# The five engine lists of a two-layer Macaron kernel, put in another order

## The chip, the cores and the metric

The kernel runs on one core of a Trainium2 chip. The metric is the device time of one launch in microseconds (us). The core has five engines, each with its own instruction list that it works off strictly in order: TensorE (PE: matmuls and transposes), VectorE (DVE), ScalarE (ACT), GpSimd (POOL) and SyncE (SP, which only issues transfers). Engines wait for one another through semaphores; whatever stands behind a waiting instruction in the same list waits too.

## The reference, cut to what matters

Two layers over 4096 tokens of width 128, in float32. Each layer is a middle block between two halves: layer 0 is a gated recurrence between two quantized linear maps, layer 1 a gated linear attention between two passes of a mixture of experts (8 routed, the best 2 per token, and a shared one):

```python
x = x + 0.5 * quant(ln(x));  x = x + recur(ln(x));  x = x + 0.5 * quant(ln(x))     # layer 0
x = x + 0.5 * experts(ln(x)); x = x + attend(ln(x)); x = x + 0.5 * experts(ln(x))   # layer 1
# recur
t  = rmsnorm(x) ; xb = causal_depthwise_conv(t @ Wx)
r, i = sigmoid(xb @ Wa), sigmoid(xb @ Wi)
a  = exp(-8 * softplus(lam) * r)
h  = scan(a, sqrt(max(1 - a*a, 1e-12)) * (i * xb))
h1 = x + (h * gelu(t @ Wy)) @ Wo
y  = h1 + (gelu(u @ Wg) * (u @ Wu)) @ Wd          # u = rmsnorm(h1)
# quant: x rounded to int8 by row, times the int8 weight, scaled, plus bias
# attend: state = state * g_t + k_t v_t^T ; o_t = q_t state ; out = o @ Wo + bo
# experts: (silu(x @ Wg.T) * (x @ Wu.T)) @ Wd.T, top 2 of 8, weighted, plus a shared one
```

## The kernel before, in words

The tokens are eight units (`u` = 0 to 7) of 512 tokens (4 tiles of 128). All of `x` stays in on-chip memory. The kernel is written as small steps, each a function named `<step>_<engine>`, and the order of the steps on each engine is written out in five blocks at the end of the kernel (lines 1486 on): `block.sync`, `vector`, `scalar`, `gpsimd`, `tensor`. Steps of many units and phases are interleaved there. The waits are inside the steps, so the order of a list changes nothing of what is computed; it decides what queues behind what. Letters of the steps:

- `k_`: constants and loads. `k_masks` turns masks to bytes on ACT, `k_split` splits the quantized weight on POOL.
- `q_` (u, p): the quantized map, pass p. `q_stats`, `q_limits`, `q_mom`, `q_par`, `q_scale`, `q_whole` and `q_out` on DVE, `q_root` and `q_bias` on POOL, `q_turn` and `q_mul` on PE, `q_copy` on ACT.
- `f_` (u): the recurrence block. On POOL `f_root`, `f_rstd`, `f_apply` (normalized x into h1, four instructions), `f_b` (the scan's input), `f_xh`, `f_root2`; on DVE `f_mom`, `f_conv`, `f_scan` (waits for `f_b`), `f_hy`; the rest on PE and ACT.
- `m_` (u, j): its feed-forward part. `g_` (u): the attention, with seven `g_level` steps on PE and DVE; `g_bias` on POOL adds a bias to `x`, `g_root` a power for the norm, `g_gate` a gate on ACT, `g_first` starts the levels.
- `r_` (u, p): the router. `r_slot` gives each token its place; `r_scatter` (POOL, four steps of two indirect transfers) writes the tokens, sorted by expert, to `rows_by_expert` in HBM. `e_` (u, p): the shared expert.
- `x_` (p, j): the routed experts, tile j of 71 in each pass; pass 0 is before the attention, pass 1 after it. The lists give p first for these, as in `x_hid_vector(dve, 0, j)`. `t_load` and `t_weights` (SP) fetch the tile's tokens (`tin`, 65 KB, ring of 12) and weights (`twt`, 256 KB, ring of 4). `x_io j` on PE first does the down projection of tile j-5 and then transposes tile j. `x_up j` is the up and gate projection, `x_silu` and `x_out` are on ACT, `x_hid` is the product on DVE, and `t_store` (POOL) scatters the result to `rows_done`. From tile 49 on, `x_dst` (DVE, 128x1, line 1113) first works out where a tile's rows go.
- The tiles come in waves that start at tiles 0, 9, 25, 41 and 49: `table p,w` on DVE computes which experts the tiles of wave w belong to, and `t_load` of its first tile waits for it and for the scatters of the units of that wave. `away` and `taken` are small tables.
- `t_stored`, `c_fetch` (SP, 512 KB a unit) and `c_add` (DVE) bring the results back and add them to `x`; `o_store` writes the output. `x_up 70`, for example, is tile 70 of the pass spoken of.

The step `x_hid`, on whose queueing much depends (lines 1116 to 1122):

```python
            dve.wait_ge(s_tsil, g + 1)
            if g >= TURNS:
                dve.wait_ge(s_tdn, g - TURNS + 1)
            dve.tensor_tensor(thidt[g % TURNS][:, :, :].rearrange("p j c -> p (j c)"), tsil[g % TURNS][:, :],
                              bank[UP_BANKS[p][j]][:, INNER:2 * INNER], ALU.mult).then_inc(s_thid, 1)
```

## Time and profile before

| | us |
| --- | --- |
| median of 3 runs | 793.06 (793.04 to 793.74) |
| span of the profiled execution (first to last instruction) | 692.3 |
| whole time of the profiled execution | not recorded; the median is 100.8 above the span |
| busy in the span: PE / DVE / POOL / ACT | 600.1 / 497.2 / 419.3 / 387.7 |
| mean granted TensorE clock | 0.972 of full |

Busy time is the union of the instructions of an engine. An engine of 87% can still be the bound for long, and one of 61% can be it for a stretch; so the rows below are read by stretches of the span.

### The profile page before, as it was taken

To read this page: it belongs to the slowest core of one execution; us is meant where nothing else is said; L and a number is where in the kernel's file an instruction comes from. 1 tells how busy PE (TensorE), PEld (TensorE's weight loads), DVE (VectorE), ACT (ScalarE), POOL (GpSimd) and SP (SyncE) were. 2 spreads that over 40 slices of the span, in tenths; PEclk is the share of its full clock that TensorE was granted. 3 is DMA by queue.
4 is the path that set the end of the run, shared out by engine and by line. 5 is a ranking of instruction groups with operands and counts; after the bars stand their busy time and mean duration, and the time that the engine had idled before them with its cause. 6 is when DMAs were issued, how large, how long until landed. Compare 5 with 4: busy or idle time off the path is not lost.

```text
span 692.3 us, 14370 instructions
## 1 busy us (share of the span) xinstructions
PE 600.1 (87%) x4124; PEld 476.3 (69%) x4124; DVE 497.2 (72%) x1721; ACT 387.7 (56%) x1019; POOL 419.3 (61%) x445
## 2 busy tenths in 40 slices
PE   0366999999989998999897899999999999978974
PEld 0224565655666797888696686769879989857863
DVE  7997999978998865557224798989877766553335
ACT  2395968988766545444353728466565355533541
POOL 5276696488567777567643614553776575775552
PEclk9996999999999999999999999999999999999997
DMA  7999000001033355666768600124216556566796
GB/s 258 410 411 371 0 1 1 1 0 32 13 99 94 97 156 161 186 193 180 211 176 245 235 6 1 35 66 131 74 43 172 153 151 177 161 182 189 231 297 232
DMA packets 60125, 100.97 MB, mean 146 GB/s; under 512 B 10288, under 2 KB 28592, under 8 KB 59792
## 3 DMA queue, kind: packets, MB, share of 16 engines
q1 hardware_dynamic: 50832, 81.52, 38.5%
q0 software_dynamic: 8640, 17.84, 7.4%
q8 instruction: 35, 0.57, 0.4%
q10 hardware_dynamic: 576, 0.69, 0.3%
q14 instruction: 42, 0.34, 0.2%
HBM read 61.79 MB, written 38.23 MB: 144 GB/s over the span
## 4 chain that ended last, share of the span: by engine, by line
PE 43%; DVE 13%; DMA 9%; issue 6%; POOL 3%; SPq 2%; ACT 2%; POOLq 0%; DVEq 0%; ACTq 0%
PE bank L1083 13%; PE bank L1058 6%; PE bank L1296 5%; DMA tin<-rows_by_expert 3%; PE bank L969 3%; PE bank L955 3%; PE bank L944 2%; DMA hid<-rows_done 2%; DMA rows_done<-tout,tdst 2%; PE bank L1064 2%; DMA rows_done<-tout,tin 1%; POOL rows_by_expert L840 1%; DVE qt L417 1%; PE bank L312 1%; PE bank L307 1%
## 5 line engine op out<-in xcount | busy, mean ns | idle before, releaser
L840 POOL DMA_INDIRECT rows_by_expert<-xx,sidx x128 | 128.1, 1001 | 72.2 <-issue 34.0
L1083 PE MATMUL bank<-tint,twt 128*128 128x128 f32 x1136 | 151.8, 282 | 6.0 <-DVE thidt L1121 3.4
L1083 PEld LDWEIGHTS bank<-tint,twt 128*128 128x128 f32 x1136 | 141.1, 196 | 22.0 <-issue 12.3
L1132 POOL DMA_INDIRECT rows_done<-tout,tin x98 | 96.3, 983 | 57.5 <-ACT tout L1107 34.8
L1121 DVE TENSOR_TENSOR thidt<-tsil,bank 128x256 f32<-128x256 f32 x142 | 58.2, 418 | 95.8 <-ACT tsil L1099 74.1
L1099 ACT ACTIVATE tsil<-bank 128x256 f32<-128x256 f32 x142 | 53.9, 384 | 89.9 <-PE bank L1083 88.4
L1058 PE MATMUL bank<-e_dn,thidt 128*128 x568 | 90.6, 286 | 15.5 <-DVE thidt L1121 7.3
L1058 PEld LDWEIGHTS bank<-e_dn,thidt 128*128 128x128 f32 x568 | 76.8, 195 | 25.2 <-issue 24.8
L1107 ACT ACTIVATE tout<-bank,tin 128x128 f32<-128x128 f32 x142 | 50.2, 366 | 62.9 <-PE bank L1064 43.7
L1132 POOL DMA_INDIRECT rows_done<-tout,tdst x44 | 43.7, 993 | 49.0 <-ACT tout L1107 35.9
L1296 PEld LDWEIGHTS bank<-bufA,bufB 128*127 128x127 f32 (+6 forms) x448 | 47.7, 176 | 11.6 <-issue 6.7
L1296 PE MATMUL bank<-bufA,bufB 128*127 128x127 f32 (+6 forms) x448 | 52.2, 263 | 3.7 <-DVE bufA L1272 1.8
L1092 ACT ACTIVATE tint<-bank 128x128 f32<-128x128 f32 x142 | 37.1, 274 | 27.6 <-PE bank L1064 27.3
L1064 PE MATMUL bank<-consts,tin 128*128 128x128 f32 x142 | 39.5, 282 | 6.4 <-DMA tin<-rows_by_expert 6.4
L687 PE MATMUL bank<-ut,w_gu 128*128 128x512 f32 x64 | 34.4, 620 | 1.7 <-DVE hid L696 1.7
L673 PE MATMUL bank<-ut,w_gu 128*128 128x512 f32 x64 | 34.5, 621 | 1.0 <-DVE x L709 1.0
L955 PE MATMUL bank<-xtr,s_gu 128*128 128x512 f32 x64 | 34.0, 614 | 0.9 <-ACT egate L951 0.9
L944 PE MATMUL bank<-xtr,s_gu 128*128 128x512 f32 x64 | 33.3, 603 | 0.4 <-DVE carry L809 0.3
L969 PEld LDWEIGHTS bank<-e_dn,ehid 128*128 128x128 f32 x256 | 30.1, 192 | 3.1 <-DVE ehid L963 1.7
L969 PE MATMUL bank<-e_dn,ehid 128*128 128x128 f32 x256 | 31.4, 276 | 0.8 <-DVE ehid L963 0.8
L963 DVE TENSOR_TENSOR ehid<-egate,bank 128x512 f32<-128x512 f32 x32 | 21.9, 684 | 13.2 <-PE bank L955 8.4
L951 ACT ACTIVATE egate<-bank 128x512 f32<-128x512 f32 x32 | 19.1, 596 | 20.5 <-PE bank L944 20.4
(272 smaller groups left out, 1331.0 us busy)
## 6 DMA issues: line engine op xcount, KB each, us to landing
twt<-moe_gu SPq DMA_DIRECT2D x142, 256.0 KB
rows_by_expert<-tout SPq DMA_DIRECT2D x25, 715.0 KB, 20.0
tin<-rows_by_expert SPq DMA_DIRECT2D x142, 65.0 KB, 2.6
hid<-rows_done SPq DMA_DIRECT2D x12, 512.0 KB, 5.5
x<-x_in SPq DMA_DIRECT2D x8, 256.0 KB, 4.4
rows_by_expert<-xx,sidx POOLq DMA_INDIRECT x128
out<-x SPq DMA_DIRECT2D x8, 256.0 KB, 3.9
rows_done<-tout,tin POOLq DMA_INDIRECT x98
```

The source lines that it names most:

```text
L840: pool.indirect_dma_start(out=rows_by_expert, out_offset=bass.IndirectOffsetOnAxis(ap=sidx[h][:, k:k + 1], axis=0), in_=xx[h][:, r, t, :], ...
L944: pe.matmul(bank[E_BANKS[p]][:, :], s_gu[:, 0, j * P:(j + 1) * P], xtr[u % 2][:, :], start=True, stop=True).then_inc(s_sg, 1)
L955: pe.matmul(bank[E_BANKS[p]][:, :], s_gu[:, 1, j * P:(j + 1) * P], xtr[u % 2][:, :], start=True, stop=True).then_inc(s_su, 1)
L969: m = pe.matmul(bank[E_BANKS[p]][:, t * P:(t + 1) * P], ehid[u % 2][:, j, t * P:(t + 1) * P], e_dn[:, SHARED, j, :], start=(j == 0), stop= ...
L1058: m = pe.matmul(bank[b][:, P:2 * P], thidt[g % TURNS][:, c, :], e_dn[:, expert_pe[j], c, :], start=(c == 0), stop=(c == IJ - 1))
L1064: pe.transpose(bank[b][:, 0:P], tin[g % RING][:, 0:D], ident).then_inc(s_tt, 1)
L1083: m = pe.matmul(bank[UP_BANKS[p][j]][:, c * P:(c + 1) * P], weights[:, c * P:(c + 1) * P], tint[g % TURNS][:, :], start=True, stop=True)
L1099: act.activation(tsil[g % TURNS][:, :], bank[UP_BANKS[p][j]][:, 0:INNER], ACT.Silu).then_inc(s_tsil, 1)
L1107: act.activation(tout[:, g % RING, :], bank[IO_BANKS[p][j + LAG_DOWN]][:, P:2 * P], ACT.Copy, scale=tin[g % RING][:, ROW_SCORE:ROW_SCORE + ...
L1121: dve.tensor_tensor(thidt[g % TURNS][:, :, :].rearrange("p j c -> p (j c)"), tsil[g % TURNS][:, :], bank[UP_BANKS[p][j]][:, INNER:2 * INNE ...
L1132: pool.indirect_dma_start(out=rows_done, out_offset=bass.IndirectOffsetOnAxis(ap=dst, axis=0), in_=tout[:, g % RING, :], in_offset=None).t ...
L1296: m = pe.matmul(gb(u, lv % 2)[0:P - w, c * P + w:(c + 1) * P], bufB[h][:, c * P:(c + 1) * P - w], bufA[h][:, c * P + w:(c + 1) * P], start ...
```

## The change

The steps, their waits and their buffers are the same: each of the five lists holds the same steps as before. Only their order is new: SP 316 steps, DVE 636, POOL 293, PE 704, ACT 745. Most move by one to five places; 2 on SP, 45 on DVE, 7 on POOL, 22 on PE and 47 on ACT move by more. The order was planned with the durations of single instructions and with transfers taken at their 85th percentile. The diff has some 3,200 lines; here are the places that the prediction speaks of, in the order SP (end of the first pass, end of the second), DVE (table of the first pass, turn of the passes, end), POOL (head, 300 to 390 us), PE (second pass, tiles 45 to 49) and ACT (286 us).

```diff
             c_fetch_sync(sp_, 0, 0)
             c_fetch_sync(sp_, 1, 0)
-            for j in range(65, 67):
+            t_load_sync(sp_, 0, 66)
+            c_fetch_sync(sp_, 2, 0)
+            for j in range(67, 69):
                 t_load_sync(sp_, 0, j)
-            t_weights_sync(sp_, 0, 65)
-            for j in range(67, 70):
-                t_load_sync(sp_, 0, j)
-            for j in range(66, 69):
+            for j in range(64, 68):
                 t_weights_sync(sp_, 0, j)
+            t_load_sync(sp_, 0, 69)
+            c_fetch_sync(sp_, 3, 0)
+            t_weights_sync(sp_, 0, 68)
+            c_fetch_sync(sp_, 4, 0)
             t_load_sync(sp_, 0, 70)
-            c_fetch_sync(sp_, 2, 0)
-            c_fetch_sync(sp_, 3, 0)
...
+            t_load_sync(sp_, 1, 66)
+            t_weights_sync(sp_, 1, 65)
+            t_load_sync(sp_, 1, 67)
             t_weights_sync(sp_, 1, 66)
+            t_load_sync(sp_, 1, 68)
+            t_weights_sync(sp_, 1, 67)
+            t_load_sync(sp_, 1, 69)
+            t_weights_sync(sp_, 1, 68)
             t_stored_sync(sp_, 1, 0)
             c_fetch_sync(sp_, 0, 1)
-            for j in range(68, 71):
-                t_load_sync(sp_, 1, j)
-            for j in range(67, 70):
-                t_weights_sync(sp_, 1, j)
+            t_load_sync(sp_, 1, 70)
             c_fetch_sync(sp_, 1, 1)
             c_fetch_sync(sp_, 2, 1)
-            t_weights_sync(sp_, 1, 70)
             c_fetch_sync(sp_, 3, 1)
             c_fetch_sync(sp_, 4, 1)
             c_fetch_sync(sp_, 5, 1)
+            for j in range(69, 71):
+                t_weights_sync(sp_, 1, j)
+            o_store_sync(sp_, 0)
+            o_store_sync(sp_, 1)
             t_stored_sync(sp_, 1, 6)
             c_fetch_sync(sp_, 6, 1)
-            o_store_sync(sp_, 0)
-            o_store_sync(sp_, 1)
-            o_store_sync(sp_, 2)
             t_stored_sync(sp_, 1, 7)
             c_fetch_sync(sp_, 7, 1)
+            o_store_sync(sp_, 2)
             o_store_sync(sp_, 3)
...
-            for j in range(29, 33):
+            for j in range(28, 30):
                 x_hid_vector(dve, 0, j)
             e_hid_vector(dve, 6, 0, 0)
-            for j in range(33, 35):
+            r_slot_vector(dve, 7, 0)
+            table_vector(dve, 0, 4)
+            for j in range(30, 33):
                 x_hid_vector(dve, 0, j)
-            table_vector(dve, 0, 4)
-            x_hid_vector(dve, 0, 35)
             e_hid_vector(dve, 6, 0, 1)
-            for j in range(36, 40):
-                x_hid_vector(dve, 0, j)
+            x_hid_vector(dve, 0, 33)
...
-            g_stats_vector(dve, 2)
-            for j in range(67, 69):
-                x_dst_vector(dve, 0, j)
             c_add_vector(dve, 3, 0)
             g_stats_vector(dve, 3)
-            x_dst_vector(dve, 0, 69)
             c_add_vector(dve, 4, 0)
-            for j in range(67, 69):
-                x_hid_vector(dve, 0, j)
+            x_hid_vector(dve, 0, 67)
+            g_stats_vector(dve, 4)
+            x_hid_vector(dve, 0, 68)
+            g_stats_vector(dve, 2)
             g_mom_vector(dve, 1)
             g_value_vector(dve, 0)
             g_first_vector(dve, 0)
@@ -2086,26 +2066,29 @@
             g_level_vector(dve, 1, 2)
             g_level_vector(dve, 0, 3)
             g_level_vector(dve, 1, 3)
+            x_dst_vector(dve, 0, 65)
             g_level_vector(dve, 0, 4)
             g_level_vector(dve, 1, 4)
-            x_hid_vector(dve, 0, 69)
             g_level_vector(dve, 0, 5)
-            x_dst_vector(dve, 0, 70)
             g_level_vector(dve, 1, 5)
             g_level_vector(dve, 0, 6)
             g_level_vector(dve, 1, 6)
-            x_hid_vector(dve, 0, 70)
-            g_stats_vector(dve, 4)
...
-            for j in range(62, 68):
+            for j in range(61, 64):
+                x_hid_vector(dve, 1, j)
+            for j in range(64, 67):
                 x_dst_vector(dve, 1, j)
+            for j in range(64, 66):
+                x_hid_vector(dve, 1, j)
+            for j in range(67, 71):
+                x_dst_vector(dve, 1, j)
+            for j in range(66, 71):
+                x_hid_vector(dve, 1, j)
             c_add_vector(dve, 0, 1)
-            for j in range(64, 67):
-                x_hid_vector(dve, 1, j)
             c_add_vector(dve, 1, 1)
-            for j in range(68, 70):
-                x_dst_vector(dve, 1, j)
-            for j in range(67, 69):
-                x_hid_vector(dve, 1, j)
             c_add_vector(dve, 2, 1)
-            for j in range(69, 71):
-                x_hid_vector(dve, 1, j)
-            x_dst_vector(dve, 1, 70)
+            e_hid_vector(dve, 7, 1, 1)
             c_add_vector(dve, 3, 1)
-            e_hid_vector(dve, 7, 1, 1)
...
             k_first_gpsimd(pool)
             q_root1_gpsimd(pool, 0)
+            k_split_gpsimd(pool)
             q_root1_gpsimd(pool, 1)
             q_bias_gpsimd(pool, 0, 0)
-            k_split_gpsimd(pool)
             q_bias_gpsimd(pool, 1, 0)
             f_root_gpsimd(pool, 0)
             q_root_gpsimd(pool, 1, 0)
             q_root_gpsimd(pool, 2, 0)
             q_bias_gpsimd(pool, 2, 0)
-            q_bias_gpsimd(pool, 3, 0)
             f_rstd_gpsimd(pool, 0)
             f_apply_gpsimd(pool, 1)
+            q_bias_gpsimd(pool, 3, 0)
             f_apply_gpsimd(pool, 0)
             f_b_gpsimd(pool, 0)
             f_root_gpsimd(pool, 1)
+            q_bias_gpsimd(pool, 4, 0)
             f_b_gpsimd(pool, 1)
+            f_root2_gpsimd(pool, 0)
+            f_root2_gpsimd(pool, 1)
+            f_rstd_gpsimd(pool, 1)
+            q_root_gpsimd(pool, 3, 0)
+            q_bias_gpsimd(pool, 5, 0)
             f_xh_gpsimd(pool, 0)
...
+            for j in range(31, 38):
                 t_store_gpsimd(pool, 0, j)
-            r_scatter_gpsimd(pool, 7, 0, 1)
             r_scatter_gpsimd(pool, 7, 0, 2)
             r_scatter_gpsimd(pool, 7, 0, 3)
-            for j in range(37, 61):
+            for j in range(38, 62):
                 t_store_gpsimd(pool, 0, j)
             g_root_gpsimd(pool, 0)
-            for j in range(61, 65):
+            for j in range(62, 64):
                 t_store_gpsimd(pool, 0, j)
             g_bias_gpsimd(pool, 0)
             g_bias_gpsimd(pool, 1)
-            for j in range(65, 67):
+            for j in range(64, 66):
                 t_store_gpsimd(pool, 0, j)
...
-            x_up_tensor(pe, 1, 44)
-            x_io_tensor(pe, 1, 48)
             x_up_tensor(pe, 1, 45)
+            for j in range(47, 49):
+                x_io_tensor(pe, 1, j)
+            x_up_tensor(pe, 1, 46)
             x_io_tensor(pe, 1, 49)
-            x_up_tensor(pe, 1, 46)
+            x_up_tensor(pe, 1, 47)
             x_io_tensor(pe, 1, 50)
-            x_up_tensor(pe, 1, 47)
-            for j in range(51, 53):
-                x_io_tensor(pe, 1, j)
...
                 x_silu_scalar(act, 0, j)
-            x_out_scalar(act, 0, 18)
-            for j in range(23, 25):
+            for j in range(21, 23):
                 x_in_scalar(act, 0, j)
+            x_out_scalar(act, 0, 16)
+            e_silu_scalar(act, 5, 0, 0)
             x_silu_scalar(act, 0, 21)
+            r_tanh_scalar(act, 6, 0)
+            x_silu_scalar(act, 0, 22)
+            x_in_scalar(act, 0, 23)
+            for j in range(17, 20):
+                x_out_scalar(act, 0, j)
             r_apply_scalar(act, 7, 0)
```

## Rows read from the trace of the kernel before

**Rows 1.** Windows of the whole span: busy time of each engine.
```profile
core 0: us, PE busy (x) PEld busy (x) DVE busy (x) ACT busy (x) POOL busy (x), PEclk, DMA share, GB/s
0.00:70.00 70.00, 29.67 (x141) 17.77 (x142) 57.60 (x216) 35.79 (x73) 35.98 (x56) 0.90 0.92 358
70.00:225.00 155.00, 148.30 (x796) 93.61 (x796) 139.28 (x443) 122.77 (x261) 109.21 (x109) 0.98 0.09 27
225.00:345.00 120.00, 110.90 (x846) 95.83 (x845) 71.25 (x275) 56.60 (x179) 84.70 (x88) 0.99 0.60 169
...
400.00:600.00 200.00, 195.42 (x1498) 166.80 (x1497) 160.75 (x578) 110.09 (x311) 113.58 (x117) 1.00 0.34 98
...
650.00:693.00 43.00, 26.58 (x192) 23.58 (x191) 18.16 (x44) 12.63 (x41) 16.62 (x18) 0.90 0.76 255
```

**Rows 2.** Timeline of POOL near 319 us: start, duration, instruction, idle before.
```profile
319.30 0.95 POOL L1132 DMA_INDIRECT rows_done<-tout,tin  x1 [0.30 <-issue]
```

**Rows 3.** Groups by line, ACT: count, busy us, mean ns, idle before.
```profile
L577 ACT ACT_TABLE_LOAD x6 | 7.7, 1283 | 0.1
```

**Rows 4.** Timeline of POOL, 37 to 55 us.
```profile
37.92 1.28 POOL L425 TENSOR_TENSOR x<-x,half_qb 128x512 f32<-128x512 f32 x1
42.57 1.27 POOL L425 TENSOR_TENSOR x<-x,half_qb 128x512 f32<-128x512 f32 x1 [3.37 <-DVE qt L417]
43.79 1.83 POOL L339 TENSOR_TENSOR lf_rstd<-lf_ve,neg_half 128x8 f32<-128x8 f32 x1
45.73 7.43 POOL L619 TENSOR_SCALAR h<-x,lf_mean,lf_rstd 128x128 f32<-128x128 f32 x8
53.13 1.26 POOL L589 TENSOR_TENSOR bufB<-bufD,bufB 128x512 f32<-128x512 f32 x1
```

**Rows 5.** Timeline of DVE, 51 to 58 us.
```profile
51.20 0.16 DVE L474 TENSOR_SCALAR ms<-lf_var 128x8 f32<-128x8 f32 x1
54.42 1.27 DVE L597 TENSOR_TENSOR_SCAN bufE<-bufA,bufB 128x256 f32<-128x256 f32 x2 [3.06 <-POOL bufB L589]
...
56.95 0.86 DVE L318 BATCH_NORM_STATS2 lq_stats<-x 128x6 f32<-128x128 f32 x4
```

**Rows 6.** Timeline of POOL, 289 us.
```profile
289.88 0.96 POOL L1132 DMA_INDIRECT rows_done<-tout,tin  x1 [3.48 <-ACT tout L1107]
```

**Rows 7.** Timeline of ACT, 288 us (two `x_out` steps).
```profile
288.70 0.81 ACT L1107 ACTIVATE tout<-bank,tin 128x128 f32<-128x128 f32 x2
```

**Rows 8.** Timeline of DVE, 305 to 318 us.
```profile
305.83 0.74 DVE L1121 TENSOR_TENSOR thidt<-tsil,bank 128x256 f32<-128x256 f32 x2
...
311.64 0.16 DVE L873 TENSOR_TENSOR cnt<-carry,consts 128x8 f32<-128x8 f32 x1
...
317.37 0.24 DVE L895 SCALAR_TENSOR_TENSOR rtab<-stab,base,consts 128x22 int32<-128x22 f32 x1
```

**Rows 9.** Timeline of ACT, 312 us (`x_out 30` and `31`).
```profile
312.06 0.62 ACT L1107 ACTIVATE tout<-bank,tin 128x128 f32<-128x128 f32 x2
```

**Rows 10.** Tile `tdst`: duration in ns, min/median/max, first and last start.
```profile
L1113 DVE TENSOR_TENSOR tdst<-tin,away_of x44: 143/152/2570, 344.1 to 678.6; 128x1 int32<-128x1 int32 x44
```

**Rows 11.** Timeline of POOL, 391 us.
```profile
390.86 2.52 POOL L1194 TENSOR_TENSOR x<-x,rows 128x512 f32<-128x512 f32 x2
```

**Rows 12.** Timeline of PE, 628 to 631 us.
```profile
628.77 0.33 PE L1064 MATMUL bank<-consts,tin 128*128 128x128 f32 x1 [1.91 <-DMA tin<-rows_by_expert]
628.93 1.23 PE L1083 MATMUL bank<-tint,twt 128*128 128x128 f32 x8
```

**Rows 13.** Timeline of DVE, 672 to 690 us.
```profile
672.13 0.69 DVE L1161 TENSOR_TENSOR x<-x,hid 128x512 f32<-128x512 f32 x1 [5.45 <-DMA hid<-rows_done]
...
678.28 0.42 DVE L1121 TENSOR_TENSOR thidt<-tsil,bank 128x256 f32<-128x256 f32 x1 [1.68 <-PE bank L1058]
...
688.41 0.69 DVE L1161 TENSOR_TENSOR x<-x,bufC 128x512 f32<-128x512 f32 x1 [2.53 <-DMA bufD<-rows_done]
```

**Rows 14.** Timeline of SP, 664 us; then the page's DMA issues.
```profile
664.37 0.33 SPq L1029 DMA_DIRECT2D twt<-moe_gu  x1
664.75 0.90 SPq L1156 DMA_DIRECT2D hid<-rows_done  x2
...
twt<-moe_gu SPq DMA_DIRECT2D x142, 256.0 KB
...
hid<-rows_done SPq DMA_DIRECT2D x12, 512.0 KB, 5.5
```

**Rows 15.** Windows, 670 to 675 us, columns as in rows 1.
```profile
670.00:675.00 5.00, 1.99 (x15) 1.80 (x14) 2.81 (x8) 1.12 (x4) 2.14 (x2) 0.91 0.99 364
```

More of the change, by code:

```diff
@@ L2096, in _ @@
             g_level_vector(dve, 1, 6)
-            x_hid_vector(dve, 0, 70)
-            g_stats_vector(dve, 4)
+            for j in range(69, 71):
+                x_hid_vector(dve, 0, j)
+            for j in range(66, 70):
+                x_dst_vector(dve, 0, j)
+            c_add_vector(dve, 5, 0)
+            r_start_vector(dve, 1)
             g_add_vector(dve, 0)
@@ L2508, in _ @@
             r_scatter_gpsimd(pool, 6, 1, 3)
-            for j in range(28, 38):
+            for j in range(30, 38):
                 t_store_gpsimd(pool, 1, j)
@@ L2711, in _ @@
             e_up_tensor(pe, 2, 0, 1)
-            for j in range(5, 7):
+            for j in range(4, 6):
                 x_io_tensor(pe, 0, j)
@@ L2715, in _ @@
             e_down_tensor(pe, 2, 0)
-            x_io_tensor(pe, 0, 7)
+            for j in range(6, 8):
+                x_io_tensor(pe, 0, j)
             r_turn_tensor(pe, 4, 0)
@@ L3108, in _ @@
             x_up_tensor(pe, 1, 27)
-            x_io_tensor(pe, 1, 29)
+            for j in range(29, 31):
+                x_io_tensor(pe, 1, j)
             r_turn_tensor(pe, 6, 1)
@@ L3112, in _ @@
             r_logits_tensor(pe, 6, 1)
-            x_io_tensor(pe, 1, 30)
+            x_io_tensor(pe, 1, 31)
             x_up_tensor(pe, 1, 29)
-            for j in range(31, 33):
+            for j in range(32, 34):
                 x_io_tensor(pe, 1, j)
@@ L3408, in _ @@
             r_apply_scalar(act, 5, 0)
-            for j in range(8, 10):
-                x_in_scalar(act, 0, j)
+            x_in_scalar(act, 0, 8)
+            q_copy_scalar(act, 6, 1)
             x_out_scalar(act, 0, 4)
@@ new lines, in _ @@
+            x_in_scalar(act, 0, 11)
+            for j in range(7, 9):
+                x_out_scalar(act, 0, j)
+            x_in_scalar(act, 0, 12)
+            e_silu_scalar(act, 4, 0, 1)
+            for j in range(9, 12):
+                x_silu_scalar(act, 0, j)
+            r_tanh_scalar(act, 5, 0)
+            x_silu_scalar(act, 0, 12)
+            for j in range(13, 15):
+                x_in_scalar(act, 0, j)
+            x_out_scalar(act, 0, 9)
+            for j in range(15, 17):
+                x_in_scalar(act, 0, j)
@@ L3485, in _ @@
+            x_in_scalar(act, 0, 32)
+            for j in range(28, 32):
                 x_silu_scalar(act, 0, j)
@@ L3509, in _ @@
             x_silu_scalar(act, 0, 36)
-            for j in range(39, 41):
+            for j in range(38, 40):
                 x_in_scalar(act, 0, j)
@@ L3610, in _ @@
             g_gate_scalar(act, 1)
-            for j in range(66, 69):
+            for j in range(64, 67):
                 x_out_scalar(act, 0, j)
@@ L3760, in _ @@
[L3760 to L3762 removed]
+            for j in range(16, 19):
+                x_silu_scalar(act, 1, j)
+            x_out_scalar(act, 1, 14)
+            x_in_scalar(act, 1, 19)
+            e_silu_scalar(act, 5, 1, 0)
+            x_out_scalar(act, 1, 15)
+            for j in range(20, 22):
+                x_in_scalar(act, 1, j)
+            g_late_scalar(act, 7, 4)
+            x_silu_scalar(act, 1, 19)
+            for j in range(16, 18):
+                x_out_scalar(act, 1, j)
@@ L3803, in _ @@
-            x_out_scalar(act, 1, 26)
-            for j in range(31, 33):
-                x_in_scalar(act, 1, j)
+            for j in range(24, 26):
+                x_out_scalar(act, 1, j)
+            r_xt_scalar(act, 6, 1)
+            x_in_scalar(act, 1, 29)
+            x_silu_scalar(act, 1, 28)
+            r_tanh_scalar(act, 6, 1)
+            for j in range(30, 32):
+                x_in_scalar(act, 1, j)
+            x_out_scalar(act, 1, 26)
+            x_silu_scalar(act, 1, 29)
+            r_rows_scalar(act, 6, 1)
@@ new lines, in _ @@
+            x_silu_scalar(act, 1, 43)
+            x_in_scalar(act, 1, 46)
+            e_silu_scalar(act, 7, 1, 0)
+            x_silu_scalar(act, 1, 44)
+            x_out_scalar(act, 1, 41)
+            x_silu_scalar(act, 1, 45)
+            x_in_scalar(act, 1, 47)
+            x_out_scalar(act, 1, 42)
+            x_silu_scalar(act, 1, 46)
+            for j in range(48, 50):
+                x_in_scalar(act, 1, j)
+            for j in range(43, 45):
+                x_out_scalar(act, 1, j)
@@ new lines, in _ @@
+            x_out_scalar(act, 1, 59)
+            for j in range(61, 63):
+                x_silu_scalar(act, 1, j)
+            x_out_scalar(act, 1, 60)
+            x_in_scalar(act, 1, 65)
+            x_silu_scalar(act, 1, 63)
+            x_in_scalar(act, 1, 66)
+            for j in range(61, 63):
+                x_out_scalar(act, 1, j)
+            x_silu_scalar(act, 1, 64)
+            x_in_scalar(act, 1, 67)
+            x_out_scalar(act, 1, 63)
+            x_in_scalar(act, 1, 68)
+            x_silu_scalar(act, 1, 65)
@@ L3927, in _ @@
                 x_silu_scalar(act, 1, j)
-            for j in range(68, 71):
+            for j in range(69, 71):
                 x_out_scalar(act, 1, j)
```

1741 lines of the change are left out of this document (824 added, 917 removed).

## The prediction, made before the changed kernel was run

> **What bounds the kernel now.** I read the span in stretches first [rows 1]. A reader should look at PE and at who else is full beside it. In the first 70 us PE has 29.7 us of work and DVE 57.6: DVE sets the pace, and the PE waits. From 70 to 225 us PE (148.3 of 155) and DVE (139.3) are both nearly full. From 225 to 345 us PE is down to 110.9 of 120, and POOL is full in fact, because its 0.96 us scatters are followed by 0.30 us in which it issues the next: a period of 1.27 us, in long unbroken runs [rows 2]. From 400 to 600 us PE is busy for 195.4 of 200, so no order gains much there. In the last 43 us PE works for 26.6 us and the transfers are at 0.76 of their engines. Then I asked for single instructions at the places where an engine stands still, and compared which step stands there in the old and in the new list.
>
> Durations are of one execution with a span of 692.3 us. Its whole time is not recorded. The median of the runs is 793.1, so 100.8 us lie around the span, and I leave them as they are.
>
> **The change part by part.** The five lists hold the same steps, so no instruction is added or taken away; only queueing changes. One thing could still add work: ACT loads a function table whenever the next function is not in the current set. The loads stand in eight groups of lines, 29 in all, each of 1.283 us [rows 3]. I walked both ACT lists with the sets which the before's loads imply (Exp with Tanh, Gelu with Tanh, Silu with Tanh, Sqrt alone, Ln alone). This reproduces all 29 loads of before at their lines, and it gives 29 for the new list too. Cost 0.
>
> *Head (term 1).* On POOL the old list puts `q_bias 3` before `f_rstd 0`, `f_apply 1`, `f_apply 0` and `f_b 0`. `q_bias 3` waits for DVE, so POOL stands from 39.20 (37.92 + 1.28) to 42.57, and `f_b 0` starts at 53.13 [rows 4]. DVE finishes `f_mom 1` at 51.36 and cannot scan until 54.42 [rows 5]. The new list starts `f_rstd 0` at 39.20: plus 1.83, plus 7.43 for both `f_apply`, plus 1.27 for `q_bias 3`, now in between, gives 49.73 for `f_b 0` and 51.0 for its end. DVE gets one `q_stats` (0.86, as in [rows 5]) ahead of the scan and reaches it at 52.2 instead of 54.4: 2.2 us. Bounds: 0 (something else holds the scan) and 3.1, the whole wait. The same shift reaches `f_root 1` and `f_b 1`, and through them the PE. `k_masks`, moved to where ACT waits for `f_root 0`, and `k_split`, moved ahead of a root, lie under DVE, which is full there: 0, and if the cover is gone, their few us show in the same 2.2. The gain lasts as far as 70 to 225 us is full with unchanged work.
>
> *POOL at 286 (term 2).* `t_store 19` waits 3.48 us for `x_out 19` [rows 6], which ACT reaches only at 288.70, behind `r_apply 7` and a Silu that waits for PE [rows 7]. The new ACT list has it before `r_apply 7`. But the next on POOL is `r_scatter 6,0,0`, and its `r_slot 6` is at about 289.5 in both lists. So only one period of 1.27 leaves the full stretch, less about 0.7 by which the rank is later: gain 0.6, bounds 0 and 1.3.
>
> *Table of the last wave, first pass (term 3).* `table 0,4` holds DVE from 311.64 to 317.61; `x_hid 29` and `30` run at 305.83 [rows 8]. The new list has `e_hid 6,0,0`, `r_slot 7` and the table before `x_hid 30`: e_hid ends near 307.6 (its `e_up` is now first), slot 308.6, table 314.6, `x_hid 30` ends 315.0, which is 8.4 later than 306.6. Behind it queue `x_io 35`, `x_up 33`, and so `x_out 30`. The cover is POOL's backlog: `t_store 31` starts at 319.30 [rows 2] though `x_out 31` is done at 312.68 [rows 9], 6.6 us of store. By hand, tile by tile at PE's pace, the new order holds until `t_store 36`, which would come at 328.2 and gets its tile at 329.5. Loss 1.3; bounds 0 and 8.4 (no cover). This also delays nothing of unit 7's scatters beyond it, since these end the full stretch in both lists.
>
> *Turn of the passes (term 4).* One `x_dst` (128x1) takes 2.57 us where the median is 0.15 [rows 10], while POOL runs the two `g_bias` [rows 11]. It stands between `c_add 3` and `c_add 4`, on the way to the first `g_level`. The new list moves it and four more behind the levels. Gain at most 2.4, at least 0 if another instruction is caught; I take the middle, 1.2, because `g_gate 0` on ACT is ready only shortly before the DVE needs it. `c_fetch 2` now precedes `t_weights 64`; `x_up 64` comes later, but `x_up 65` to `68`, which set `x_hid 66` and `g_turn 0`, keep their place: 0.
>
> The Trainium skill, "SBUF — State Buffer", on engine ports, says that a DVE instruction with two SBUF inputs and a GpSimd instruction that reads SBUF exclude each other, and the second waits for the whole of the first. By this rule, `c_add`, which also has two SBUF inputs, would be caught in its place, and term 4 would be 0. The 2.57 us agree with the rule.
>
> *Second pass, last wave (term 5).* PE stands 1.91 us for a load before `x_io 49` and does `x_up 46` after it, 1.23 with its overlap [rows 12]. The new list does `x_up 46` first: 0.9 saved (a group without overlap), bounds 0 and 1.9.
>
> *Tail (term 6).* DVE waits 5.45 us for a fetch before `c_add 1`, with `x_hid 67` and `68` behind it [rows 13]. The new list has all `x_hid` first and all eight `c_add` after. So after `x_hid 70`, 14 adds, `e_hid` and `e_add` of 0.69 each, 11.0 us, come before the last `c_add`. With `x_hid 70` ending at 678.70, this would start at 689.7 instead of 688.41 [rows 13]. When is the new `x_hid 70`? SP now issues the fetches of units 0 to 5 before `t_weights 69` and `70`: 3.1 + 0.5 MB from 664.4 on [rows 14]. At 364 GB/s [rows 15] they land at 674.2, at the 255 GB/s of the last stretch [rows 1] at 678.4. With 1.9 us for `x_up`, Silu and product, `x_hid 70` ends between 676.1 and 680.3, so the last `c_add` starts between 687.1 and 691.3. Middle 689.2: loss 0.8, bounds a gain of 1.3 and a loss of 2.9. `o_store 0` and `1` now stand before the wait for the last stores, but both are through before the last store lands.
>
> All other moves are of one to five places inside full stretches. I price them at 0.
>
> Sum: 692.3 - 2.2 - 0.6 + 1.3 - 1.2 - 0.9 + 0.8 = 689.5; with 100.8 around it, **790.3 us**.
>
> **Rivals.**
> 1. *More is gained.* Every term at its good bound: 3.1 + 1.3 + 0 + 2.4 + 1.9 + 1.3 = 10.0, 783.1 us. For it: each wait named is real. Against: five independent good ends.
> 2. *The port takes term 4 back* (`c_add` caught instead): 791.5 us.
> 3. *The head gain is absorbed* between 70 and 225 us, where POOL has new late steps (`f_xh 6` behind two scatter groups, `q_bias 6` behind a root): 792.5, no change.
> 4. *Slower: DVE's table starves POOL.* Place: 308 to 334 us. If the backlog does not cover the 8.4 us, unit 7's scatters, all of the last wave and the second pass come later by up to 8.4 instead of 1.3: 797.4 us. It decides from where POOL stands more than 5.7 us there (1.3 + the 2.8 of net gain + 1.6). For it: backlog at `t_store 36` was only 1.9 us. Against: PE has 9 us of slack in the stretch and can catch up.
>
> **How the numbers follow.** A measurement of this kernel tells about 0.2%, 1.6 us. Chances: forecast (788.5 to 791.4) 0.36; rival 1 0.20; rival 2 0.10, on the edge of that bound; rival 3 0.13; rival 4 0.21. Faster is 0.36 + 0.20 and half of rival 2: 0.61. Same is the other half and rival 3, less rounding: 0.17. Slower 0.22. The range goes from rival 1 to rival 4: 783 to 797.5. The forecast's own range is 787 to 793.
>
> **What the profile after would show.** Term 1: the first scan at about 52.2, and PE's first long busy run 2 us earlier. Term 2: no hole of 3.5 on POOL near 286. Term 3: `table 0,4` near 309 with the `x_hid` of tiles 30 to 35 bunched behind it, and a POOL hole of about 1 us before unit 7's last scatters. Term 4: the 2.5 us of waiting gone, or on an add. Term 5: no wait for a load before `x_io 49`. Term 6: no wait of 5 us for a fetch between the last `x_hid`, and sixteen DVE operations in a row at the end. ACT table loads: 29. The prediction is wrong if POOL stands long before 334 us, if the middle stretches, priced at 0, shift by more than 1 us, or if the loads of the last weights are late.

## The result, and the profile after

The changed kernel took 804.2 us (median of 4 runs, 803.0 to 811.6) beside 793.4 for the kernel before: a ratio of 1.0141, 95% interval 1.0096 to 1.0187. Slower by 1.4%, where 790.3 was forecast, in a range up to 797.5. Four more comparisons on other chips gave 1.0176, 1.0104, 1.0115 and 1.0156, so the sign stands. Medians from here on leave out executions over 1.5% above the fastest of their kernel.

Three executions must be told apart before any row can be compared. The header of the page of the changed kernel, and its first group:

```profile
span 801.2 us, 14370 instructions
...
PE 634.3 (79%) x4124; PEld 501.8 (63%) x4124; DVE 504.3 (63%) x1721; ACT 383.7 (48%) x1019; POOL 414.3 (52%) x445
```

This execution took 803.0 us, so 1.8 us lie around its span, not 100.8. The kernel before, profiled again, gave 684 us (span 682.1) on one chip and 792 (span 790.0) on another. The seven chips that the experiments ran on split into two with 684 to 686 us for the kernel before (called short here) and five with medians of 794 to 800 (long); all executions on one chip are of one kind. Each chip was used for one set of runs only, so that it is the chip, and not the time of the run, is likely and not shown. The profile of [rows 1] is of the short kind and the times beside it are of the long one; on which chip it was taken is not recorded. The headers of these two profiles of before, short first, then long:

```profile
PE 594.2 (87%) x4124; PEld 472.1 (69%) x4124; DVE 496.8 (73%) x1721; ACT 387.8 (57%) x1019; POOL 418.0 (61%) x445
```

```profile
PE 629.7 (80%) x4124; PEld 496.0 (63%) x4124; DVE 495.3 (63%) x1721; ACT 385.3 (49%) x1019; POOL 417.8 (53%) x445
```

DVE, ACT and POOL do the same work; on a long chip the engines wait more. So the changed kernel on a short chip (span 697.4) is compared with the short 682.1, and the long 801.2 with the long 790.0. Windows of the changed kernel on a short chip (columns as in [rows 1]):

```profile
0.00:70.00 70.00, 32.70 (x160) 18.97 (x160) 61.18 (x222) 38.64 (x81) 35.72 (x57) 0.93 0.92 358
70.00:225.00 155.00, 146.68 (x810) 93.55 (x808) 146.62 (x454) 119.85 (x252) 110.48 (x111) 1.00 0.10 28
225.00:345.00 120.00, 112.27 (x875) 99.11 (x874) 70.46 (x265) 59.50 (x192) 86.36 (x89) 0.99 0.65 180
345.00:400.00 55.00, 46.60 (x334) 40.32 (x334) 33.91 (x102) 25.01 (x71) 21.86 (x22) 0.97 0.59 183
400.00:600.00 200.00, 191.19 (x1439) 162.41 (x1440) 156.89 (x556) 109.08 (x312) 113.90 (x119) 0.98 0.35 97
```

Read the PE column. Up to 70 us PE does 3 us more than in [rows 1]: the head did gain. From 400 to 600 us, which was 195.4 of 200 full, PE has lost 4.2 us, and its clock is at 0.98. That is the stretch whose moves the prediction priced at nothing. Starts of the same steps on short chips, from the timelines (us; the kernel before in the execution of 682.1):

| step | before | changed | difference |
| --- | --- | --- | --- |
| first scan | 54.4 | 52.2 | -2.2 |
| `r_scatter 5,0,0` | 266.7 | 262.6 | -4.1 |
| `r_scatter 7,0,3` (last of pass 0) | 327.9 | 327.0 | -0.9 |
| first `g_level` | 390.1 | 390.6 | +0.4 |
| `g_level 4,0` | 462.6 | 467.3 | +4.8 |
| `g_level 6,0` or `7,0`, whichever is first | 519.0 | 528.9 | +9.9 |
| `x_hid 60`, pass 1 | 645.6 | 657.0 | +11.4 |
| last `c_add` | 678.3 | 693.1 | +14.8 |

These two are single executions. The medians beside each other on one short chip (686.3 and 698.6) give 12.3. The execution that the prediction read, also short, reaches the first `g_level` only at 398.8, so differences before that point are no firmer than this.

**The tail.** SP, then PE, then DVE of the changed kernel on the short chip:

```profile
663.65 0.33 SPq L1156 DMA_DIRECT2D hid<-rows_done  x1
...
668.74 0.49 SPq L1154 DMA_DIRECT2D bufB<-rows_done  x1
669.93 0.87 SPq L1029 DMA_DIRECT2D twt<-moe_gu  x2
```

```profile
669.86 1.96 PE L1058 MATMUL bank<-e_dn,thidt 128*128 x12
677.35 3.75 PE L1083 MATMUL bank<-tint,twt 128*128 128x128 f32 x16 [5.53 <-issue]
```

```profile
679.85 0.42 DVE L1121 TENSOR_TENSOR thidt<-tsil,bank 128x256 f32<-128x256 f32 x1 [9.00 <-ACT tsil L1099]
681.55 0.42 DVE L1121 TENSOR_TENSOR thidt<-tsil,bank 128x256 f32<-128x256 f32 x1 [1.28 <-ACT tsil L1099]
681.89 0.69 DVE L1161 TENSOR_TENSOR x<-x,hid 128x512 f32<-128x512 f32 x1
...
693.81 0.69 DVE L1162 TENSOR_TENSOR x<-x,bufD 128x512 f32<-128x512 f32 x1
```

The last two weight loads are issued at 669.93, 6.3 us behind the first fetch. They are needed 7.4 us later: PE does `x_up 69` and `70` at 677.35, after 5.5 us idle, and the sixteen matmuls take 3.75 us where sixteen took 1.95 at full clock (at 638.67). The granted clock is 1.00 from 665 to 672 us, before the idle time, and 0.50 from 677 to 681. DVE stands 9.00 us for `x_hid 69`, and the adds follow behind `x_hid 70`. The long execution shows the same:

```profile
783.60 0.42 DVE L1121 TENSOR_TENSOR thidt<-tsil,bank 128x256 f32<-128x256 f32 x1 [9.00 <-ACT tsil L1099]
```

**DVE against POOL in the full stretch.** DVE, POOL and PE of the changed kernel on the short chip:

```profile
519.50 1.77 DVE L768 TENSOR_SCALAR probs<-probs 128x32 f32<-128x32 f32 x1 [0.29 <-ACT probs L762]
521.30 0.43 DVE L771 TENSOR_TENSOR above<-probs 128x256 f32<-128x256 f32 x1
521.76 2.19 DVE L776 TENSOR_TENSOR above<-probs 128x64 f32<-128x64 f32 x3
```

```profile
519.94 1.28 POOL L1194 TENSOR_TENSOR x<-x,rows 128x512 f32<-128x512 f32 x1
...
522.63 1.28 POOL L1194 TENSOR_TENSOR x<-x,rows 128x512 f32<-128x512 f32 x1
```

```profile
524.78 0.22 PE L790 MATMUL bank<-chosen,before_bf 128*128 128x40 bf16 x1 [2.47 <-DVE chosen L781]
```

`r_rank 4` (DVE, the router's ranking of the experts) takes 5.6 us instead of 2.0: its instructions of 0.18 and 0.40 us last 1.77 and 2.19, and each ends with one of the two `g_bias` of POOL (521.2 and 523.9). PE waits 2.47 us for it, and from 520 to 530 us its mean clock is 0.83. In the kernel before, DVE has the same step free of POOL, whose `g_bias 6` and `7` ran at 507.9:

```profile
514.62 0.18 DVE L768 TENSOR_SCALAR probs<-probs 128x32 f32<-128x32 f32 x1 [0.30 <-ACT probs L762]
514.84 0.42 DVE L771 TENSOR_TENSOR above<-probs 128x256 f32<-128x256 f32 x1
515.30 0.40 DVE L776 TENSOR_TENSOR above<-probs 128x64 f32<-128x64 f32 x3
```

The new POOL list has `t_store 2` of the second pass ahead of `g_bias 6`, and that store waits for ACT until 518.9. On long chips the same overlap is shorter: `r_rank 4` takes 4.6 us and PE stands 1.7 (long execution of 801.2).

DVE's busy time for the same 1,721 instructions is 509.9 us against 496.8 (short) and 504.3 against 495.3 (long). This sum is not the loss. The kernel with only the head new (below) has 504.4 us of DVE, nearly all of the increase, and the time of before; the one with only the second half new has 500.4. So most of the longer DVE instructions lie in the head, where they cost nothing that could be measured; which POOL instructions they meet there was not traced.

### The profile page after: what moved, and what is told of

Same layout as the page of the kernel before. It is cut to its first block, busy times and chain, and to the rows that moved or that the text cites. A ratio compares the mean times of both kernels' runs of the same rounds, so it can differ in the third digit from the quotient of the medians.

```text
span 801.2 us, 14370 instructions
## 1 busy us (share of the span) xinstructions
PE 634.3 (79%) x4124; PEld 501.8 (63%) x4124; DVE 504.3 (63%) x1721; ACT 383.7 (48%) x1019; POOL 414.3 (52%) x445
## 4 chain that ended last, share of the span: by engine, by line
PE 37%; DVE 20%; issue 12%; another core or an unknown queue 8%; ACT 4%; DMA 3%; POOL 1%; SPq 0%; DVEq 0%; ACTq 0%; POOLq 0%
PE bank L1083 13%; PE bank L1058 6%; PE bank L1296 3%; PE bank L969 2%; PE bank L955 2%; PE bank L944 2%; DMA rows_done<-tout,tdst 2%; PE bank L307 2%; PE bank L1064 2%; PE bank L312 1%; DVE thidt L1121 1%; DMA tin<-rows_by_expert 1%; DVE lr_stats L318 1%; DVE qt L417 1%
## 5 line engine op out<-in xcount | busy, mean ns | idle before, releaser
L1083 PE MATMUL bank<-tint,twt 128*128 128x128 f32 x1136 | 166.2, 298 | 35.9 <-issue 17.4
L1083 PEld LDWEIGHTS bank<-tint,twt 128*128 128x128 f32 x1136 | 153.3, 210 | 54.1 <-issue 36.7
L840 POOL DMA_INDIRECT rows_by_expert<-xx,sidx x128 | 125.0, 977 | 84.0 <-DVE xx L819 39.2
L1058 PE MATMUL bank<-e_dn,thidt 128*128 x568 | 95.8, 297 | 31.3 <-issue 19.9
L1058 PEld LDWEIGHTS bank<-e_dn,thidt 128*128 128x128 f32 x568 | 82.2, 206 | 45.8 <-issue 45.5
L1296 PE MATMUL bank<-bufA,bufB 128*127 128x127 f32 (+6 forms) x448 | 55.4, 271 | 11.6 <-DVE at L1325 9.0
L1296 PEld LDWEIGHTS bank<-bufA,bufB 128*127 128x127 f32 (+6 forms) x448 | 50.1, 183 | 19.5 <-DVE tseg L1318 9.3
L944 PE MATMUL bank<-xtr,s_gu 128*128 128x512 f32 x64 | 36.9, 661 | 9.7 <-DVE x L975 3.3
L969 PE MATMUL bank<-e_dn,ehid 128*128 128x128 f32 x256 | 33.2, 286 | 5.0 <-DVE ehid L963 4.4
L955 PE MATMUL bank<-xtr,s_gu 128*128 128x512 f32 x64 | 35.5, 637 | 2.1 <-issue 1.4
L1313 DVE TENSOR_TENSOR bufA<-bufA,tseg 128x256 f32<-128x256 f32 x56 | 23.8, 426 | 20.6 <-remote 13.5
```

The lines of the kernel that those rows point to most:

```text
L840: pool.indirect_dma_start(out=rows_by_expert, out_offset=bass.IndirectOffsetOnAxis(ap=sidx[h][:, k:k + 1], axis=0), in_=xx[h][:, r, t, :], ...
L944: pe.matmul(bank[E_BANKS[p]][:, :], s_gu[:, 0, j * P:(j + 1) * P], xtr[u % 2][:, :], start=True, stop=True).then_inc(s_sg, 1)
L955: pe.matmul(bank[E_BANKS[p]][:, :], s_gu[:, 1, j * P:(j + 1) * P], xtr[u % 2][:, :], start=True, stop=True).then_inc(s_su, 1)
L969: m = pe.matmul(bank[E_BANKS[p]][:, t * P:(t + 1) * P], ehid[u % 2][:, j, t * P:(t + 1) * P], e_dn[:, SHARED, j, :], start=(j == 0), stop= ...
L1058: m = pe.matmul(bank[b][:, P:2 * P], thidt[g % TURNS][:, c, :], e_dn[:, expert_pe[j], c, :], start=(c == 0), stop=(c == IJ - 1))
L1083: m = pe.matmul(bank[UP_BANKS[p][j]][:, c * P:(c + 1) * P], weights[:, c * P:(c + 1) * P], tint[g % TURNS][:, :], start=True, stop=True)
```

## The experiments

Three kernels cut the change by time: each takes the new order for the steps of one stretch and the old one for the rest. A fourth is the kernel before, for its profile on the same (long) chip.

> The kernel before once more, for its profile on the chip that the next three kernels run on. Theory A (two kinds of executions, set by the chip): either about 682 us of span or about 793, and the three kernels beside it are of the same kind.

It took 791.8 us, span 790.0. With an earlier profile of the same kernel (684 us) it showed the two levels of time; that run's expectation was:

> The kernel before, unchanged, for its profile alone. The profiled execution of before that the prediction was made against has a span of 692.3 us, 100.8 below the median of its times; the profiled execution of the changed kernel has a span of 801.2 and a time of 803.0, so only 1.8 us lie around a span. Theory A: the execution of 692.3 was not like the timed ones, and a second one has a span of 791, with the 100 us spread from 225 us on over waits for loads of tin. Theory B: the execution was ordinary and before's executions come in two lengths; then this span is 692 again, and the time 694.

**Only the head new** (up to 205 us):

```diff
-            q_bias_gpsimd(pool, 3, 0)
             f_rstd_gpsimd(pool, 0)
             f_apply_gpsimd(pool, 1)
+            q_bias_gpsimd(pool, 3, 0)
...
```

> New order only up to about 205 us (the stretch before the first wave of the routed experts), the order of before for the rest. By the terms of the prediction this alone gives 2.2 us less (term 1). If it is the head with its later scatters of unit 3 that costs, it is slower than before by 2 us or more.

**Only the first pass new** (205 to 396 us; lists of all engines, here DVE):

```diff
-            r_slot_vector(dve, 7, 0)
...
+            r_slot_vector(dve, 7, 0)
...
```

> The order of before up to 205 us, the new order for the steps of 205 to 396 us (first pass of the routed experts), the order of before after that. By the prediction: terms 2 and 3, 0.7 us more. If rival 4 (table 0,4 starves POOL) is what made the changed kernel slow, this one carries nearly all of its 11 us.

**Only the second half new** (from 396 us):

```diff
+            for j in range(69, 71):
+                t_weights_sync(sp_, 1, j)
...
-            t_weights_sync(sp_, 1, 70)
...
```

> The order of before up to 396 us, the new order from there on (turn of the passes, attention, second pass, tail). By the prediction: terms 4 to 6, 1.3 us less. If the new loss lies in the second pass or the tail, this one is slower by 5 us or more and the other two are not.

Ratios to before: 0.9991 (0.9948 to 1.0033), 0.9987 (0.9937 to 1.0036), 1.0150 (1.006 to 1.024). The second half carries the loss; rival 4 (the table of the first pass starves POOL) is out as its cause. The first kernel was run again on another long chip:

> New order only up to 205 us. The first scan came 2.4 us earlier in its profile, and table 0,0 1.7, but x_hid 0 only 0.5. Term 1 says 2.2 less in the whole time (ratio 0.997), the rival of absorption says 1.000.

Two executions at 791.4 and 787.9 us (two more, at 800.5 and 803.4, are over the limit) beside 795.9: too few for a ratio. The scan does come 2.2 us earlier (52.2). Whether anything of it is left at the end is open on a long chip: the interval of the first run, 0.9948 to 1.0033, holds a gain of 2.2 us (0.9972) as well as none (rival 3).

**The two weight loads.** The changed kernel with this edit, and the kernel before with the reverse one:

```diff
             t_load_sync(sp_, 1, 70)
+            for j in range(69, 71):
+                t_weights_sync(sp_, 1, j)
             c_fetch_sync(sp_, 1, 1)
...
             c_fetch_sync(sp_, 5, 1)
-            for j in range(69, 71):
-                t_weights_sync(sp_, 1, j)
```

> The changed kernel with one edit on SP: t_weights 69 and 70 of the second pass ahead of the fetches of units 1 to 5 instead of behind them. In the kernel with only the second half new, these two were issued at 772.2 us instead of 763.7 and x_up 69 ran 11.5 us later. If the tail of SP is the cause, nearly all of the loss comes back: 8 to 10 us less than the changed kernel, at or below the time of before (ratio 0.995 to 1.003). If it is the adds of DVE, or the middle of the second pass, it stays at 1.012 or more.

> The kernel before with that one edit the other way: t_weights 69 and 70 of the second pass behind the fetches of units 1 to 5. If the tail of SP is the cause: 6 to 9 us slower than before (ratio 1.008 to 1.011). If it is something else in the second half: no change.

With them, on the same long chip, the mended kernel with three adds put back among the last `x_hid`, and the changed kernel itself:

```diff
+            c_add_vector(dve, 0, 1)
             for j in range(64, 66):
                 x_hid_vector(dve, 1, j)
...
+            c_add_vector(dve, 1, 1)
             for j in range(67, 69):
                 x_hid_vector(dve, 1, j)
+            c_add_vector(dve, 2, 1)
...
```

> As the first, and on DVE the adds of units 0, 1 and 2 back among the last x_hid (before tiles 64, 67 and 69), where the kernel before has them. If the adds behind x_hid 70 are on the path, it gains up to 2.4 us on the first kernel (three adds and their reads are 4.1 us of the 11.0 behind x_hid 70); if the last add waits for unit 7's fetch anyway, it is equal to the first, or slower by what the wait for a fetch takes from x_hid 67.

> The changed kernel unchanged, for the same chip as the other three. If this chip takes about 793 us for the kernel before, 1.4 to 1.8% more than it; if it takes about 684, the tail's loss of 8 us is the same in us, and the ratio is 1.005 to 1.015.

The changed kernel and the one with the two loads ahead were run as a pair again, on another long and on a short chip:

> The changed kernel unchanged, once more, for a chip on which the kernel before takes 684 to 694 us if this is one. The tail's loss does not depend on the stalls of PE, so there it is 8 us again, less about 2 for the head and the adds: 5 to 8 us slower, ratio 1.008 to 1.012. If the new list is better matched to the short kind of execution (it was priced on a profile of that kind), as the prediction has it: 0.996. On a chip of 793 us: 1.010 to 1.018 as before.

> The changed kernel with t_weights 69 and 70 ahead of the fetches, beside the unchanged one: 5 to 8 us less than it on either kind of chip. On a chip of 684 us, where no stalls of PE blur the sum, what is left against before is the sum of terms 1 to 5 of the prediction: minus 3.6 if they hold, so a ratio of 0.995; 1.000 if they are absorbed.

> The changed kernel unchanged, beside the next one: 1.0 to 1.4 per cent slower than before on a chip of 793 us; on a chip of 684 us 5 to 8 us slower.

> The changed kernel with t_weights 69 and 70 ahead of the fetches: 7 to 13 us less than the unchanged one; against before a ratio of 0.997 to 1.003.

| chip | before | changed | weights first | gained |
| --- | --- | --- | --- | --- |
| long | 800.2 | 809.5 (1.0104) | 802.8 (1.0033) | 6.7 |
| long | 795.9 | 806.4 (1.0115) | 792.8 (0.9972) | 13.5 |
| short | 686.3 | 698.6 (1.0156) | 691.8 (1.0088) | 6.8 |

The ratios are the recorded ones and differ a little from the quotients of the medians beside them (698.6 / 686.3 would be 1.018). The reverse edit alone: 805.5, ratio 1.0055 (1.0020 to 1.0090). The three adds back: 802.9, ratio 1.0050 (1.0017 to 1.0083), no gain. Medians of long chips move by several us from run to run, so the sharper reading is inside the profiles, from the start of `x_hid 60` of the second pass to the end of the span:

| order of the tail | us, one number for each profile |
| --- | --- |
| before (6 profiles; the first two short) | 38.7, 36.6, 36.9, 36.5, 37.2, 35.3 |
| new (6; the last short), and before with the reverse edit (long) | 42.6, 43.3, 43.9, 43.5, 43.2, 40.4; 43.9 |
| new, weights first (4; the third short, the last with the edit on POOL below) | 36.1, 34.6, 36.3, 34.5 |
| new, weights first, three adds back | 38.3 |

The shortest tail with the loads last, 40.4, is longer than the longest with them ahead, 38.7. The place of the two loads costs 7.4 us between the means (42.8 and 35.4), 4.1 in the one pair of short profiles. The rest of the tail's new order (DVE with all `x_hid` first, and the lists of the other engines) gives 1.5 between means of 36.9 and 35.4 whose values overlap; one kernel for DVE alone was not run.

The two kinds of chips lose in different places. From the start of the first `g_level` to that of `x_hid 60` of the second pass (us, one number for each profile, by the order of that stretch):

| kind | order of before | new order |
| --- | --- | --- |
| short | 254.8, 255.5 | 266.4, 263.9 |
| long | 312.8, 314.0, 320.3, 315.8, 316.5 | 315.2, 314.2, 318.1, 315.6, 316.3, 324.6, 311.3, 319.2 |

On a short chip this middle loses 8.5 to 11.6 us and the tail with the loads last only 1.7 to 3.8. On a long chip the middle shows no loss in a spread of 13 us (means 315.9 and 316.8), and the tail loses 6.8 (43.3 and 36.5).

The changed kernel unchanged on one more long chip gave 1.0176 (1.0099 to 1.0252):

> The changed kernel, unchanged, in three rounds against the kernel before. In the result the two took 804 and 793 us, but a second execution of the kernel before took 684 us. Theory A: what took 793 us was the chip or its state, not the list; where the kernel before takes 684 to 694, the changed one takes 1.4% more, 695 to 703, and its waits of 5 us and more are gone. Theory B: the kernel before takes either 684 or 793, and the new lists sit at 800 always: then this is 800 beside 686, 17% slower.

**POOL off r_rank 4.** On the mended kernel:

```diff
             r_root_gpsimd(pool, 2, 1)
-            t_store_gpsimd(pool, 1, 2)
             g_bias_gpsimd(pool, 6)
-            t_store_gpsimd(pool, 1, 3)
             g_bias_gpsimd(pool, 7)
-            for j in range(4, 6):
+            for j in range(2, 6):
                 t_store_gpsimd(pool, 1, j)
```

> The changed kernel with t_weights 69 and 70 ahead of the fetches, and on POOL g_bias 6 and 7 of the attention straight behind r_root 2 (where the kernel before has them) instead of behind t_store 2 and 3 of the second pass, which wait for ACT. In the profiles of the new order they run at 518 to 523 us, on top of r_rank 4 on DVE, which then takes 5.6 us instead of 2.0, and PE stands 2.5 us for it and then runs at half clock. Theory A (DVE and POOL hold each other up): r_rank 4 takes 2.0 to 2.1 us again, the wait of 2.5 us before r_counts 4 is gone, and the time is 3 to 5 us below the kernel with the weights alone: a ratio to before of 0.998 to 1.003 on a chip of 684 us (that kernel: 1.0088 there), 0.993 to 0.998 on one of 793 (1.0033 and 0.9972 there). Theory B (r_rank 4 is long for another reason, such as the x_up that overlaps it): it still takes over 4 us, and the ratio stays.

DVE, then POOL, of its profile (a long chip):

```profile
593.57 0.18 DVE L768 TENSOR_SCALAR probs<-probs 128x32 f32<-128x32 f32 x1 [0.30 <-issue]
593.78 0.43 DVE L771 TENSOR_TENSOR above<-probs 128x256 f32<-128x256 f32 x1
594.24 0.40 DVE L776 TENSOR_TENSOR above<-probs 128x64 f32<-128x64 f32 x3
```

```profile
582.64 2.49 POOL L1194 TENSOR_TENSOR x<-x,rows 128x512 f32<-128x512 f32 x2
```

The step is back at 2.0 us: that POOL's two instructions stretch it is shown. What follows on DVE moves too. From the start of `r_rank 4` to the next first level (`g_level 6,0` or `7,0`) it takes 4.4 us in all nine profiles with the order of before there, 7.3 in the eight long ones with the new order, 9.4 and 8.1 in the two short ones, and 5.4 with this edit. The whole time was 802.4 us, ratio 1.0059 (1.0017 to 1.0101), not below the mended kernel without the edit (1.0033 and 0.9972 on other long chips). Gains of 2 to 3 us cannot be told at such intervals, so for the whole time this run decides nothing; on a short chip, where the stretch costs more, the edit was not run.

**What makes a chip long.** The kernel before with twelve pairs of waits that are already met behind each `t_weights` on SP, on a long and on a short chip. Each pair is one instruction in the trace, 1,704 more in all:

```diff
                           ).then_inc(s_wt[g % WRING], 16)
+            for _ in range(12):
+                sp_.wait_ge(s_first, 1)
+                sp_.wait_ge(s_table, 1)
```

> The kernel before with twelve waits that are already met behind each t_weights on SP (1,704 more recorded instructions, 0.03 us each on an engine that stands idle half of the time). Theory A: executions of 793 us are held up by the recording itself (7,863 of 13,100 records of semaphore updates are left in one, all losses from 200 us on, where the stalls are); then more records cost 10 us or more on such a chip, and nothing on a chip of 684. Theory B: it is not the recording; then the waits cost the same on either kind, 0 to 3 us, for the loads that SP issues up to 0.4 us later.

> The kernel of e4 once more. On a chip of 793 us: 844 again. On a chip of 684 us it is the control that e4 lacked: theory A says 684 to 688, theory B says the same 48 us more as on the other kind.

Long: 843.8 beside 795.9 us, 48 more (ratio 1.0611). Short: 713.8 beside 686.3, 27.5 more (one run). So both expectations fail as they were put: the edit costs 27 us where there are no stalls, presumably because SP issues its loads later, and a long chip adds 20. In the short profile every added wait of line 1033 lasts 0.03 us; in the long one the longest lasts 0.71.

## Why the prediction was wrong

- **The base.** "The median of the runs is 793.1, so 100.8 us lie around the span, and I leave them as they are." They do not exist: 1.8 us lie around a span. The profile was of the short kind and the times of the long one. The size of the sum was hardly touched by it, but the prediction took the difference between two kinds of executions for a constant, and a gap of 100 us was a warning to be followed up.
- **Term 1** held as a mechanism: the first scan at 52.2, as forecast. In the pair of short profiles it is 4.1 us by 267 us and gone by the first `g_level` (+0.4). By this pair rival 3 was right on the gain being absorbed, though not on the place: the gain outlived 225 us and went between 267 and 390. No interval of whole times shows it either way.
- **Term 2** priced what one execution had. The hole of 3.48 us in [rows 6] is 0.78 in the second short profile of the same kernel; its store there:

```profile
286.13 0.96 POOL L1132 DMA_INDIRECT rows_done<-tout,tin  x1 [0.78 <-ACT tout L1107]
```

- **Term 3** is not settled. Between `r_scatter 5,0,0` and `7,0,3` the changed kernel loses 3.2 us (-4.1 to -0.9; 64.4 us against 61.2), where 1.3 was the middle and 8.4 the bound. But the execution that the prediction read takes 64.7 us there with the old lists, so the 3.2 us lie within what two executions of one kernel differ by.
- **Term 4** was rival 2's. In the profile that the prediction read, `x_dst` was caught under POOL [rows 10, 11]. In the second short profile of before and in the changed kernel an add is caught instead (before first, then changed), both under the two `g_bias`:

```profile
383.09 3.00 DVE L1162 TENSOR_TENSOR x<-x,hid 128x512 f32<-128x512 f32 x1
```

```profile
381.60 2.52 DVE L1161 TENSOR_TENSOR x<-x,hid 128x512 f32<-128x512 f32 x1
```

 So with either order one instruction waits, and nothing is gained. The rule of the Trainium skill that was weighed there ("SBUF — State Buffer", "SBUF: two separate sides") gave 0 for this term, and the rows agree with it.
- **Term 5** came true and was given back. On short chips `x_hid 45` to `48` of the second pass take 10.4 us before and 6.4 after, so 4.0 are saved where 0.9 was forecast; by `x_hid 54` 2.4 of it are lost again.
- **Term 6** is the step that failed most where the result was measured. It gave a loss of 0.8, bounds -1.3 and +2.9; the profiles of long chips give +6.8 against before, the short ones +2.7 (40.4 against 38.7 and 36.6). Its order of events was right, and its parts can be measured in the six profiles with the loads last:
  - From the first fetch to `x_up 69` the sum had 9.8 to 14.0 us (3.6 MB at 364 or 255 GB/s), 11.9 in the middle. It takes 13.2 to 14.2. So the slower rate was the right one, and the middle was 1.8 too small.
  - From `x_up 69` to the end of `x_hid 70` the sum had 1.9 us. It takes 4.6 in all six: two tiles come one behind the other, and PE, idle for 5.5 us before, does them at half clock (3.75 us instead of 1.95).
  - The 11.0 us behind `x_hid 70` held (11.1 to 11.5).
  - The first fetch, taken at 10.9 us behind `x_hid 60`, comes at 9.3 on long chips and 6.7 on the short one. That takes back 1.6 to 4.2 us.
  - The norm was one execution's tail, 38.7 us, the longest of six (mean 36.9). That hid about 2 us.
- **"All other moves … I price them at 0."** This is the second failed step, the larger one on a short chip, and the text named its own test (a shift of over 1 us). There the middle shifts by 9.5 us between the first `g_level` and the first level of units 6 and 7. 5.2 of them come behind `g_level 4,0`, where `r_rank 4` is stretched by 3.6 us and PE stands 2.5; the other 4.3, up to 467 us, were not traced to one move. With the weights mended, 5.5 us are left against before on the short chip (1.0088), 8.3 between the two profiles; there the tail is no longer than before (36.3 against 36.6), and all of it is in the middle.
- The 29 table loads of ACT held (29 after, 1.283 us each).

The loss is thus settled for the tail: the place of the two loads was changed in both directions on a long chip, and in one direction on a short one. For the middle, which matters on short chips, the stretch is known and the moves only in part. None of these kernels is shown to beat the kernel before: 0.9972 (0.9937 to 1.0006) was the best, and the same kernel has 1.0033 and 1.0088 on other chips.

## What to carry to other kernels

Ahead of the last items of work, a load that the chain needs goes before the bulk transfers that only the end needs: the price is all the bytes ahead of it, at the slower of the rates seen, plus what PE does slower after standing still (here 3.75 us instead of 1.95). A wait or a long instruction that is seen once in one profile is a sample; a second profile of the same kernel shows whether the change can remove it. And when lists are reordered in stretches that are full, look for pairs of DVE and POOL instructions that newly overlap: the work is equal, its duration is not. Whether that costs time depends on the place; a sum of busy time over the whole span does not tell.

## What the hardware showed

- **One kernel, two levels of time**: 684 to 686 us on two chips, 794 to 800 on five. Up to 200 us the profiles agree within 3 us. Behind that, on a long chip, consumers see the results of PE late though its records are on time. In the long profile of before, `e_down` of PE ends at 251.9 and DVE waits for it until 256.92:

```profile
249.97 1.95 PE L969 MATMUL bank<-e_dn,ehid 128*128 128x128 f32 x16
```

```profile
256.92 0.69 DVE L975 SCALAR_TENSOR_TENSOR x<-bank,x 128x512 f32<-128x512 f32 x1 [4.58 <-remote]
```

 SP's register moves show it without PE. On the long chip (first) the longest lasts 702 ns, on the short one (second) 37:

```profile
L1020 SPq MOVE tin<-rows_by_expert x142: 3/29/702, 198.5 to 761.6; - x142
```

```profile
L1020 SPq MOVE tin<-rows_by_expert x142: 29/29/37, 200.3 to 654.2; - x142
```

 The trace of the long one holds 7,863 records of semaphore updates where the short one holds 13,100, nearly all of the difference after 200 us (up to there 1,619 and 1,742); with 1,704 more instructions the numbers are 8,516 and 13,097. The stalls, the lost records and the extra 20 us of the kernel with more records go together, which speaks for the recording of the profile as the cause. It is not shown: an idle engine with many records, which could not delay a load, was not measured. The Trainium skill ("NOTIFIC — the notification-queue block", "Overflow: three behaviours, one of which stalls the engine") describes a mode in which a full ring stalls the engine that writes to it; no run here shows which mode was set.
- **A DVE instruction caught beside POOL's ends when POOL's has ended.** DVE instructions of 0.18 and 0.40 us became 1.77 and 2.19 and ended at 521.3 and 523.9 us, as POOL's of 1.28 did (521.2 and 523.9); an add of 0.69 became 2.52 and ended 0.6 us behind POOL's two of 2.50. Which instruction is caught is a matter of a few tenths of a us, and so differs between two executions of one kernel.
